# Key spreading by DMA, and gate product and two normalisations on GpSimd, in a two-layer attention and FFN kernel

## What is computed

```
x = x + L0_xattn(layernorm(x), ctx)   # banded attention of 8 heads over the 256 columns, gated
x = x + L0_ffn(layernorm(x))          # 32 of 64 rows of each sequence, chosen by score; gelu
x = x + L1_xattn(layernorm(x), ctx)   # 32 query heads, 8 key and value heads
x = x + L1_ffn(layernorm(x))          # relu squared, expert matrix scaled by top-2 logits, layernorm
```

```
qkv = x^T @ w_in.T + b_in ; q, k, v = 8 heads of 8
scores = q k^T / sqrt(8), band |i - j| <= 64 ; attn = softmax(scores)
o = (attn v) @ w_out.T + b_out          # transposed back
y = relu(o) * ctx                       # the gate product
out = w_ct^T y + b_ct
```

## Time and profile before

| | |
|---|---|
| median of 3 runs | 362.23 us (362.06 to 362.73) |
| profiled execution | 362.1 us, span 360.4 us |
| PE busy | 320.2 us, 89% of the span |
| DVE busy | 256.2 us, 71% |
| ACT busy | 208.1 us, 58% |
| POOL busy | 192.7 us, 53% |
| DMA | 12.16 MB in 10150 packets, nearly all in the first tenth of the span |
| costliest DVE group | L1110, 256 masked maxima, 79.1 us |

### The profile page before, as it was taken

How to read it: one execution, slowest core, us unless ns; L and a number is a source line. 1 busy time by engine, 2 the same in 40 slices (tenths; PEclk the granted TensorE clock), 3 DMA queues, 4 the chain that set the end, 5 groups by cost and what they waited for, 6 DMA issues and landing times.

```text
span 360.4 us, 7398 instructions
## 1 busy us (share of the span) xinstructions
PE 320.2 (89%) x2258; PEld 252.3 (70%) x2258; DVE 256.2 (71%) x935; ACT 208.1 (58%) x438; POOL 192.7 (53%) x287
## 2 busy tenths in 40 slices
PE   0689999779798898999999999899999999999993
PEld 0467768567576666767777777777777767888892
DVE  5899999999989899988323615576478846661364
ACT  2639888759687695967841341467577865213210
POOL 4757988758767585856602431515152543244733
PEclk9859999999999999999999999999999999999997
DMA  7996000000000000000000000000000000000011
GB/s 220 363 373 227 1 3 3 1 2 3 1 2 0 3 3 1 3 2 2 2 2 0 0 2 0 1 2 0 2 3 0 2 0 3 0 31 15 1 38 37
DMA packets 10150, 12.16 MB, mean 34 GB/s; under 512 B 1920, under 2 KB 8832, under 8 KB 10112
## 3 DMA queue, kind: packets, MB, share of 16 engines
q1 hardware_dynamic: 9536, 11.36, 9.2%
q10 hardware_dynamic: 576, 0.33, 0.4%
HBM read 10.64 MB, written 1.05 MB: 32 GB/s over the span
## 4 chain that ended last, share of the span: by engine, by line
PE 58%; DVE 27%; issue 8%; ACT 3%; POOL 2%; DMA 1%; POOLq 0%; DVEq 0%; SPq 0%; ACTq 0%
DVE masked L1110 10%; PE S L666 6%; PE S L339 5%; PE O L377 4%; PE ST L690 4%; PE S L472 4%; PE ST L361 4%; PE S L608 2%; PE S L536 2%; PE PJ L449 2%; PE PJ L579 2%; PE O L623 2%; PE PJ L310 2%; DVE st L1072 2%; PE XB L597 2%
## 5 line engine op out<-in xcount | busy, mean ns | idle before, releaser
L1110 DVE CUSTOM_DVE_ANT_0 masked<-S,band 128x192 bf16<-128x192 f32 x256 | 79.1, 353 | 8.4 <-PE S L339 7.3
L785 ACT ACTIVATE ex<-ST 128x384 f32<-128x384 f32 x128 | 62.2, 489 | 14.0 <-PE ST L361 13.4
L339 PE MATMUL S<-qk 128*128 128x384 f32 x128 | 53.5, 424 | 10.2 <-DVE mw L1110 8.1
L948 POOL TENSOR_SCALAR rstd<-mv 128x1 f32<-128x1 f32 x40 | 11.8, 294 | 94.2 <-DVE mv L1074 94.0
L960 POOL TENSOR_TENSOR qk<-kp,kmask 128x1024 fp32r<-128x1024 f32 x24 | 46.3, 1934 | 5.0 <-DVE kp L1208 4.9
L361 PE MATMUL ST<-qk 128*128 128x192 f32 x256 | 48.7, 273 | 0.0
L361 PEld LDWEIGHTS ST<-qk 128*128 128x128 f32 x256 | 44.5, 189 | 1.9 <-issue 1.2
L339 PEld LDWEIGHTS S<-qk 128*128 128x128 f32 x128 | 24.8, 195 | 23.3 <-issue 16.1
L1254 DVE TENSOR_REDUCE mw<-S 128x8 f32<-128x512 f32 x32 | 22.0, 687 | 17.9 <-PE S L536 17.8
L751 ACT ACTIVATE hs<-PJ,sb,cols 128x512 fp32r<-128x512 f32 x29 | 22.5, 777 | 20.6 <-PE PJ L311 20.1
L377 PE MATMUL O<-ex,v 128*32 128x192 f32 x512 | 34.2, 338 | 0.0
(11 more groups left out here) (178 smaller groups left out, 757.9 us busy)
## 6 DMA issues: line engine op xcount, KB each, us to landing
w<-in_w SPq DMA_DIRECT2D x2, 1024.0 KB, 10.1
cx<-in_cx SPq DMA_DIRECT2D x1, 1024.0 KB, 7.9
cxT<-in_cxT SPq DMA_DIRECT2D x1, 1024.0 KB, 9.6
up<-in_up SPq DMA_DIRECT2D x1, 1024.0 KB, 10.9
down<-in_down SPq DMA_DIRECT2D x1, 1024.0 KB, 11.8
out<-x SPq DMA_DIRECT2D x8, 128.0 KB, 1.7
x<-in_x SPq DMA_DIRECT2D x1, 768.0 KB, 5.6
vecs<-in_vecs SPq DMA_DIRECT2D x1, 640.0 KB, 8.0
```

The source lines that it names most:

```text
L339: mm(out, r32(qp[:, t % 2, g, b, P * c:P * c + P]), r32(mv_), start=True, stop=True).then_inc(s["pe_s"], 1)
L785: A(ex[:, (n // 2) % 4, 2 * w:2 * w + 2, :], ST[n % 2][:, 0:2 * WIN].rearrange("p (h k) -> p h k", h=2), ACT.Exp, scale=SCALE).then_inc(s[ ...
L1110: last = V.tensor_tensor_reduce(out=masked[:, n % 2, h, :], in0=S[n % 2][:, WIN * h:WIN * h + WIN], in1=band[:, c, :], scale=1.0, scalar=N ...
```

## The change

- Keys of tiles 2 to 7: SP issues, for each tile, 24 DMAs from `kp` to `kb`, one for each sequence b, head j and copy r of the rows, each of 8 partitions by 2 groups by 256 columns (16 KB). The rows of other heads and the ones at row 96 stay as the masked products of tiles 0 and 1 left them in the two buffers. The DMAs of b = 0 wait for the second key mix of the tile and for the transposed scores that last read this half of the buffer, those of b = 1 for theirs. PE waits for all twelve of a sequence (`ld_kb0`, `ld_kb1`) where it waited for `pool_kb` and `act_kb`; DVE's key mix of the next tile waits for all 24.
- GpSimd and ACT spread keys for tiles 0 and 1 only.
- The normalisation into `xn` of tiles 1 to 7 is on GpSimd in slot 4 (was DVE, slot 9).
- The gate product is on GpSimd in slot 6 (was DVE, slot 6); PE's matmul with `wc0` is in slot 8 (was 7) and DVE's addition to x in slot 9 (was 8).
- The second normalisation is on GpSimd in slot 14 (was DVE, slot 15). The one copy into `spread` (L1148) is in slot 13 of turn 2 (was slot 15).

```diff
--- before.py
+++ after.py
@@ -145,7 +145,7 @@
                  "dve_w dve_band dve_ln dve_xn dve_xl dve_mix dve_max dve_rc dve_on dve_x dve_zero "
-                 "pool_var pool_rstd pool_mw dve_y pool_kb pool_sel pool_zero act_kb dve_spread ld_sel "
+                 "pool_var pool_rstd pool_mw pool_y pool_xn pool_fxn pool_kb pool_sel pool_zero act_kb ld_kb0 ld_kb1 dve_spread ld_sel "
                  "f_ln f_rstd f_xn f_sc f_cmp f_sel fp_sT fp_x fa_x fp_up fa_up fp_dn f_dn fp_sc f_x "
@@ -163,6 +163,10 @@
             return r // 8, (r % 8) // 4, (r % 4) // 2, r % 2
+
+        def normalised(t):
+
+            return (s["dve_xn"], 1) if t == 0 else (s["pool_xn"], t)
@@ -234,6 +238,7 @@
         KA = {11: 0, 12: 1, 15: 2, 18: 3}
+        KB_DMA = 16 * 12
@@ -282,6 +287,14 @@
                 load(dst, src, "ld_late")
+            for t in range(2, TILES):
+                sp.wait_ge(s["dve_mix"], 4 * t + 2)
+                for b in range(2):
+                    sp.wait_ge(s["pe_st"], UNITS * (t - 2) + 8 * b + 8)
+                    for j in range(4):
+                        for r in range(3):
+                            rows = slice(32 * r + 8 * j, 32 * r + 8 * j + 8)
+                            sp.dma_start(kb[rows, t % 2, :, j, b, :], kp[rows, :, b, :]).then_inc(s[f"ld_kb{b}"], 16)
             ov = a["out"].rearrange("(t p) c -> p t c", p=P)
@@ -316,7 +329,7 @@
                     pe.wait_ge(s["ld_small"], 64)
-                pe.wait_ge(s["dve_xn"], t + 1)
+                pe.wait_ge(*normalised(t))
                 for c in range(2):
@@ -326,7 +339,9 @@
                     b, g, c, w = parts(r)
-                    if (b, g) == (1, 1):
+                    if t >= 2:
+                        pe.wait_ge(s[f"ld_kb{b}"], KB_DMA * (t - 1))
+                    elif (b, g) == (1, 1):
                         pe.wait_ge(s["act_kb"], t + 1)
@@ -400,8 +415,8 @@
                         mm(XB[:, 0:T], wo0[:, :], onT[:, t % 2, :], start=True, stop=True).then_inc(s["pe_out"], 1)
-                    if l == 7:
-                        pe.wait_ge(s["dve_y"], t + 1)
+                    if l == 8:
+                        pe.wait_ge(s["pool_y"], t + 1)
                         mm(XB[:, 0:T], wc0[:, :], yr[:, 1, :], start=True, stop=True).then_inc(s["pe_wct"], 1)
@@ -724,7 +739,7 @@
                         if t >= 1:
-                            act.wait_ge(s["dve_y"], t)
+                            act.wait_ge(s["pool_y"], t)
                         A(yr[:, 0, :], XB[:, 0:T], ACT.Relu, bias=bcol[:, 3:4]).then_inc(s["act_relu"], 1)
@@ -751,13 +766,11 @@
                 for t, j in ((T_ + 1, KA.get(l)), (T_, KA.get(l + UNITS))):
-                    if j is not None and 0 <= t < TILES:
+                    if j is not None and 0 <= t < 2:
                         if j == 0:
...
                                 act.wait_ge(s["ld_small"], 64)
-                            if t >= 2:
-                                act.wait_ge(s["pe_st"], UNITS * (t - 1))
                         last = A(r32(kb[:, t % 2, 1, j, 1, :]), kp[:, 1, 1, :], ACT.Copy, scale=kmask[:, j:j + 1])
@@ -770,7 +783,7 @@
                 if l == 14 and 0 <= t < TILES:
-                    act.wait_ge(s["dve_xn"], t + 1)
+                    act.wait_ge(*normalised(t))
                     if t >= 1:
@@ -955,18 +968,36 @@
                     pool.wait_ge(s["ld_small"], 64)
-                if t >= 2:
-                    pool.wait_ge(s["pe_st"], UNITS * (t - 2) + 8 * b + 4 * g + 4)
                 G.tensor_tensor(r32(kb[:, t % 2, g, :, b, :]), kp[:, g, b:b + 1, :].to_broadcast([P, 4, T]),
                                 kmask[:, :, None].to_broadcast([P, 4, T]), ALU.mult).then_inc(s["pool_kb"], 1)
+
+            def normalise(dst, t, name):
+                G.tensor_scalar(dst, x[:, t, :], mv[:, t, 0:1], rstd[:, t:t + 1], ALU.subtract, ALU.mult).then_inc(s[name], 1)
...
                     inv_std(t, "dve_ln", 2 * t + 2, "pool_rstd")
+                if l == 4 and 1 <= t < TILES:
+                    pool.wait_ge(s["pool_rstd"], t + 1)
+                    if t >= 2:
+                        pool.wait_ge(s["pe_v"], t - 1)
+                    normalise(xn[:, t % 2, :], t, "pool_xn")
                 t = T_ - 2
+                if l == 6 and 0 <= t < TILES:
+                    pool.wait_ge(s["act_relu"], t + 1)
+                    if t == 0:
+                        pool.wait_ge(s["ld_rest"], 64)
+                    if t >= 1:
+                        pool.wait_ge(s["pe_wct"], t)
+                    G.tensor_tensor(yr[:, 1, :], yr[:, 0, :], cx[:, t, :], ALU.mult).then_inc(s["pool_y"], 1)
                 if l == 13 and 0 <= t < TILES:
                     inv_std(t, "f_ln", 2 * t + 2, "f_rstd")
+                if l == 14 and 0 <= t < TILES:
+                    pool.wait_ge(s["f_rstd"], t + 1)
+                    if t == 0:
+                        pool.wait_ge(s["dve_spread"], 1)
+                    normalise(x_norm(t), t, "pool_fxn")
                 if T_ >= 0:
@@ -985,7 +1016,7 @@
                 t = T_ + 1
-                if l in KB and 0 <= t < TILES:
+                if l in KB and 0 <= t < 2:
                     keys(t, *KB[l])
@@ -1126,14 +1157,7 @@
                 if 0 <= t < TILES:
-                    if l == 6:
-                        dve.wait_ge(s["act_relu"], t + 1)
-                        if t == 0:
-                            dve.wait_ge(s["ld_rest"], 64)
-                        if t >= 1:
-                            dve.wait_ge(s["pe_wct"], t)
-                        V.tensor_tensor(yr[:, 1, :], yr[:, 0, :], cx[:, t, :], ALU.mult).then_inc(s["dve_y"], 1)
-                    if l == 8:
+                    if l == 9:
                         dve.wait_ge(s["pe_wct"], t + 1)
@@ -1141,21 +1165,17 @@
                         stats(t, x[:, t, :], "f_ln", 2 * t)
-                    if l == 15:
-                        dve.wait_ge(s["f_rstd"], t + 1)
-                        if t == 0:
-                            dve.wait_ge(s["ld_sel"], 96)
-                            V.tensor_copy(r32(spread[:, :, :, :].rearrange("p a b c -> p (a b c)")), hT[:, 0:2, :].rearrange("p a b -> p (a b)"))\
-                                .then_inc(s["dve_spread"], 1)
-                            dve.wait_ge(s["dve_spread"], 1)
-                        V.tensor_scalar(x_norm(t), x[:, t, :], mv[:, t, 0:1], rstd[:, t:t + 1], ALU.subtract, ALU.mult).then_inc(s["f_xn"], 1)
+                    if l == 13 and t == 0:
+                        dve.wait_ge(s["ld_sel"], 96)
+                        V.tensor_copy(r32(spread[:, :, :, :].rearrange("p a b c -> p (a b c)")), hT[:, 0:2, :].rearrange("p a b -> p (a b)"))\
+                            .then_inc(s["dve_spread"], 1)
                 t = T_ - 3
...
                     if l == 0:
-                        dve.wait_ge(s["f_xn"], 2 * t + 1)
+                        dve.wait_ge(s["pool_fxn"], t + 1)
                         V.tensor_tensor_reduce(out=cmp[:, 0:2, :].rearrange("p a b -> p (a b)"), in0=x_norm(t), in1=vecs[:, 0, :], scale=1.0,
                                                scalar=0.0, op0=ALU.mult, op1=ALU.add, accum_out=sc[:, t:t + 1]).then_inc(s["f_xn"], 1)
-                        dve.wait_ge(s["f_xn"], 2 * t + 2)
+                        dve.wait_ge(s["f_xn"], t + 1)
                         V.tensor_scalar(sc[:, t:t + 1], sc[:, t:t + 1], br[:, 0:1], None, ALU.add).then_inc(s["f_sc"], 1)
@@ -1179,11 +1199,6 @@
                         stats(t, x[:, t, :], "dve_ln", 2 * t)
-                    if l == 9 and t >= 1:
-                        dve.wait_ge(s["pool_rstd"], t + 1)
-                        if t >= 2:
-                            dve.wait_ge(s["pe_v"], t - 1)
-                        normalise(xn[:, t % 2, :], t, "dve_xn")
                 t = T_ + 1
@@ -1198,10 +1213,13 @@
                     dve.wait_ge(s["act_hs"], m + 1)
-                    if n < 2 and t >= 1:
+                    if n < 2 and t in (1, 2):
                         dve.wait_ge(s["pool_kb"], 3 * t)
...
                             dve.wait_ge(s["act_kb"], t)
+                    if n < 2 and t >= 3:
+                        dve.wait_ge(s["ld_kb0"], KB_DMA * (t - 2))
+                        dve.wait_ge(s["ld_kb1"], KB_DMA * (t - 2))
                     if n >= 2 and t >= 2:
...
                     dst = (qp[:, t % 2, g, :, :] if n >= 2 else kp[:, g, :, :]).rearrange("p b q -> p (b q)")
```

## The result

The changed kernel takes 383.37 us (median of 4 runs, 381.07 to 385.73), the kernel before 362.17 us (a fourth run is added to the three of the table of before, which gave 362.23). The ratio is 1.058, with a 95% interval of 1.051 to 1.066. The prediction was 352.7 us, range 347 to 361: wrong in sign.

A forecast was written before the change was run, and what follows sets the result against it. DVE was taken to bound turns 0 to 7, PE the rest. DVE's relief of 11.4 + 4.5 - 1.8 = 14.1 us, less 4.1 to PE and 0.5 for DMAs, gave 9.5 us: 352.7 us, range 347 to 361.

The forecast's parts named there:

- What bounds: DVE's order of work sets the pace of turns 0 to 7, PE's the rest; gain only in turns 0 to 7.
- Work removed from DVE, and PE as the next limit: Turns 0 to 7: 11.4 us of instructions and 4.5 us of slowing leave DVE; 4.1 us of it goes to PE.
- Work added on GpSimd: Product and normalisations at 0.74 us each, 2.2 us a turn; blocking DVE costs 0.3 us a turn, 1.8 us in all.
- The key spread by DMA: SP's queue: issues 0.47 us apart, landing 1.7 us, first twelve ready in 7.0 us, second twelve delay nobody; costs 0.5 us.
- The slower rival: SP's queue becomes the bound before a tile's first score matmul; gain gone at 0.69 us an issue, 367 to 377 us; chance 0.14.
- the likelier rival: SBUF-to-SBUF DMAs land at 3.2 us or issue in 0.55; first score matmuls wait, 357 to 361 us; chance 0.17.
- The late landing rival: Landing at 3.2 us or issue of 0.55: each tile's score matmul waits 0.7 to 1.6 us more, 357 to 361; chance 0.17.
- PE takes the gain: PE's in-order waits on DVE stay, a turn ends at 20.2 us instead of 19.4; gain halved, 357 us; chance 0.16.
- more gain: DVE's L1156 and L1169 fall to their minima and PE keeps nothing: about 16 us gained, 346 us; chance 0.08.

The follow-up runs named there:

- half_dmas: The changed kernel with only the DMAs of heads 0 and 1, 12 a tile instead of 24, the other copies left out; 351.4 us, ratio 0.970.
- hybrid_moves_late: The changed kernel with DMAs for the second sequence only, GpSimd spreading the first in slot 6 instead of 5; 351.8 us, ratio 0.972.
- dma_alone: The kernel before with the key spread of tiles 2 to 7 by DMA and nothing else changed; 382.5 us, ratio 1.056.
- moves_alone: The changed kernel with its key spread put back on GpSimd and ACT for all tiles; 364.3 us, ratio 1.006.
- kp_double: The changed kernel with `kp` double buffered by tile, so the key mix waits for DMAs of two tiles back; 369.7 us, ratio 1.019.
- dma_probe: The kernel before with 35 extra DMAs of seven shapes on the idle SP queue, single and three in a row; 362.2 us (one run).
- two_queues: The changed kernel with `kp` double buffered and four of a tile's first twelve DMAs issued by ACT instead of SP; 369.8 us, ratio 1.021.

## Why the prediction was wrong

**What bounds.** Right: turns 0 to 7 were DVE's, nothing behind them moved.

**Work removed from DVE, and PE as the next limit.** The time that came of it was right. I had 19 to 20 us for turns 3 to 6 and 352.7 us; with the DMA deadlines kept they are 19.2 to 19.4 us and 351.4 us (half_dmas), 18.7 to 19.9 and 351.8 (hybrid_moves_late). L1156 went from a median of 0.66 to 0.42 us (L1176 in the changed kernel). The size of the relief was not right: I had 14.1 us, and DVE's busy time fell by 20.3 us in the changed kernel, of which 10.8 come with the DMAs alone (245.4 us in dma_alone). That the time still came out fits the step to PE: turn 4 of half_dmas has PE busy for 17.96 of 19.30 us, 93% where I had assumed 95, and DVE for 16.83. No run tests by itself that PE sets the pace there, so the closeness of 351.4 to 352.7 is in part luck.

**Work added on GpSimd.** The ceiling of 0.74 us was wrong for the normalisations: with one tensor operand and two scalars a partition they took 1.24 us each, longer than the product of two tensors (0.73). It was harmless in the change, since GpSimd has room (13.2 of 24.7 us in turn 4). The 0.3 us a turn for what it blocks was not measured by itself; with the key spread gone from GpSimd nothing in half_dmas speaks for more. Where GpSimd still spreads keys in slot 5, the selection took 1.8 to 1.9 us in turns 3 to 5 (moves_alone), against 0.93 before.

**The key spread by DMA.** This step failed, in both its numbers and in its structure. The issues were 0.73 us apart, not 0.47, because I took the figure from DMAs with an HBM source; nor would the stores of the kernel before, with an SBUF source and 0.33 us an issue, have shown it, for none of its DMAs goes from SBUF to SBUF. The landing was 2.03 us, not 1.7. At these the first twelve are ready 11 x 0.73 + 2.03 = 10.1 us after the mix, as measured, 1.9 us beyond the 8.2. And the second twelve, which I dismissed with 3.3 us to spare, are ready after 17.2 + 2.03 = 19.2 us against 15.9: 3.3 us too late, in front of DVE's next key mix. That mix leads to the second one, and that to the next 24 issues, so the lateness does not end as a wait that later slack absorbs; it becomes the period. Both steps count: from the forecast of 352.7 us to kp_double's 369.7 are 17.0 us, which stand there with the loop gone and the first twelve DMAs late, and from there to 383.4 are the 13.7 us of the loop.

**The slower rival.** It named the queue and its deciding point, issues 0.69 us apart, and had 0.14. Priced by its own formula at 0.73 us apart and 2.03 us of landing it gives about 367, near kp_double's 369.7 and not 383: it looked at the first score matmul only. Of the 16 us between, the loop through `kp` makes 13.7. The unknown issue was bounded by 0.55 in the likelier rival, with no row for it.

**The late landing rival** was not it: 2.03 us lies near the low end of 1.7 to 3.2, and its other condition, an issue of 0.55 us, pointed the right way but not far enough. **PE takes the gain** and **more gain** could not show behind the queue.

## What to carry to other kernels

When work goes to a DMA queue, count every issue of an iteration, add the landing and the way back to the first issue of the next, and compare that sum with the period; a single-buffered source turns a late last DMA into the period, while a missed first deadline costs only itself, here 1.9 us a turn. Before such a change, measure one DMA of the very kind (source and destination, shape) on an idle queue, for a row of another kind bounds nothing. And when an engine is relieved, look at what it will now run beside: a DVE instruction that arrives earlier can land behind a long GpSimd instruction, and a shift of one slot in the order may be worth as much as the work removed.

## What the runs showed of the hardware

- The issue of a DMA on SP's queue took 0.59 to 0.70 us from SBUF to SBUF and 0.28 to 0.39 us from HBM to SBUF, for 8 to 128 partitions (second single ones of dma_probe), and 0.33 us from SBUF to HBM (the output stores, 128 KB). An SBUF-to-SBUF DMA of 16 KB landed 2.03 us after its issue began.
- ACT took 3.09 us for four issues from SBUF to SBUF and stood idle for 2.81 us of it; SP issued 0.72 us apart beside it (two_queues).
- GpSimd normalised 128x256 with two scalars a partition in 1.24 us, DVE in 0.41; a product of two tensors took 0.73 there.
- A DVE selection of 0.35 us took 1.82 us beside a GpSimd product of 1.90 us and ended with it. The Trainium skill ("SBUF — State Buffer", section "Who interferes with whom") says that DVE in one of its two-port modes, which `tensor_scalar` can enter, and GpSimd shut each other out for the whole of the instruction that was issued first. These rows agree: GpSimd started 0.16 us earlier, and the two ended within 0.08 us of each other (100.88 and 100.96); in which mode DVE ran, the trace does not show.
- PE was granted 0.80 and 0.93 of its full clock (2.4 GHz) in turns 3 and 4 of the changed kernel, in which it waited repeatedly, and 1.00 in the same turns of hybrid_moves_late. The loss that comes of the clock was not measured by itself. Of the loop of 24.6 us, only the stretch from the start of the first key mix to the end of the second has PE in it: 5.2 to 6.1 us in turns 3 to 6 of the changed kernel and 5.1 to 5.7 us in hybrid_moves_late. The means are 5.7 and 5.3, so an estimate from these rows gives the clock at most some 0.4 us a turn of the loop.
